# Attention probabilities transposed by VectorE blocks and DMAs inside SBUF, with contexts and outputs one step behind the scores

## The reference, cut to what matters

```python
def _cross_attention(q_in, kv_in, wq, bq, wk, bk, wv, bv, wo, bo, bias_k, bias_v):
    qh = (q_in @ wq + bq).reshape(b, q_len, H, K)
    kh = (kv_in @ wk + bk).reshape(b, t, H, K)
    vh = (kv_in @ wv + bv).reshape(b, t, H, K)
    kh = concatenate([kh, bias_k]); vh = concatenate([vh, bias_v])   # one learned key and value
    logits = jnp.einsum('bqhk,bthk->bhqt', qh, kh) / scale
    weights = jax.nn.softmax(logits, axis=-1)
    ctx = jnp.einsum('bhqt,bthk->bqhk', weights, vh).reshape(b, q_len, H * K)
    return ctx @ wo + bo
```

## Time and profile before

| | |
|---|---|
| median of 3 runs | 567.76 us |
| span of the profiled execution | 565.1 us; no time of its own is listed for it, so 2.7 us between it and the median stand for what lies around it |
| TensorE busy | 548.0 us, 97% |
| VectorE, ScalarE, GpSimd busy | 408.8, 315.1, 330.1 us (72%, 56%, 58%) |
| one step in the loop | 31.96 us |
| the chain that ended last | TensorE 82%, VectorE 11% |

### The profile page before, as it was taken

One profiled execution on the slowest core, in us unless ns is written; L12 is line 12 of the kernel. 1 busy time (PEld: TensorE's weight loads), 2 busy tenths in 40 slices (PEclk: granted clock), 3 DMA queues, 4 the chain that ended last, 5 costly groups with the idle time before them and its releaser, 6 DMA issues.

```text
span 565.1 us, 11067 instructions
## 1 busy us (share of the span) xinstructions
PE 548.0 (97%) x3665; PEld 492.8 (87%) x3665; DVE 408.8 (72%) x802; ACT 315.1 (56%) x707; POOL 330.1 (58%) x380
## 2 busy tenths in 40 slices
PE   7999999999999999999899999999999999999887
PEld 5979899898989899898879989898998989897787
DVE  3995776858586776858787685958768685858884
ACT  3475564747475564737266473746556474756432
POOL 3765655738364664837947393646557383746730
PEclk8999999999999999999999999999999999999999
DMA  7403030302102030301203020120203020000101
GB/s 240 128 22 73 19 74 0 78 15 56 37 22 70 18 75 0 74 20 54 77 19 94 1 74 19 43 50 19 74 0 92 1 71 22 0 19 2 38 1 38
DMA packets 26398, 25.85 MB, mean 46 GB/s; under 512 B 1530, under 2 KB 26254, under 8 KB 26382
## 3 DMA queue, kind: packets, MB, share of 16 engines
q1 hardware_dynamic: 26382, 25.64, 16.8%
HBM read 25.11 MB, written 0.52 MB: 45 GB/s over the span
## 4 chain that ended last, share of the span: by engine, by line
PE 82%; DVE 11%; issue 3%; DMA 1%; ACT 1%; POOL 0%; SPq 0%; DVEq 0%; ACTq 0%; POOLq 0%
PE ring L855 44%; PE ps_ctx L855 20%; PE acc L855 10%; PE ring L893 8%; DVE row_max L634 5%; DVE shift L640 2%; DMA probs<-ctx_in 1%; DVE z_sb L681 1%; ACT probs L469 1%; DVE x_sb L662 1%; DVE k_hi L841 0%; DVE cols L729 0%; DVE h_full L688 0%; DVE bn L670 0%; PE ring L930 0%
## 5 line engine op out<-in xcount | busy, mean ns | idle before, releaser
L336 POOL TENSOR_TENSOR v_lo<-v_sum,v_hi 128x512 fp32r<-128x512 f32 x64 | 82.2, 1295 | 129.1 <-ACT v_hi L448 127.3
L343 POOL TENSOR_SCALAR probs<-probs,inv 128x512 f32<-128x512 f32 x128 | 87.2, 694 | 63.9 <-DVE inv L656 63.9
L469 ACT ACTIVATE probs<-ring,shift 128x512 f32<-128x512 f32 x113 | 77.4, 685 | 32.3 <-DVE shift L640 28.7
L634 DVE TENSOR_REDUCE row_max<-ring 128x1 f32<-128x512 f32 x113 | 75.9, 685 | 11.6 <-PE ring L855 11.6
L448 ACT ACTIVATE v_hi<-v_sum 128x512 fp32r<-128x512 f32 x64 | 40.4, 632 | 77.4 <-DVE v_sum L611 77.4
L618 DVE TENSOR_TENSOR pT_lo<-ring,pT_hi 128x512 fp32r<-128x512 f32 x126 | 81.2, 684 | 3.0 <-ACT pT_hi L455 0.5
L455 ACT ACTIVATE pT_hi<-ring 128x512 fp32r<-128x512 f32 x126 | 69.9, 594 | 0.6 <-PE ring L893 0.5
L855 PE MATMUL ps_ctx<-pT_lo,v_hi 128*128 128x256 f32 x236 | 67.6, 286 | 0.0
L893 PE MATMUL ring<-ident,probs 128*128 128x128 f32 x504 | 65.8, 273 | 1.0 <-POOL probs L343 0.7
L855 PE MATMUL ps_ctx<-pT_hi,v_lo 128*128 128x256 f32 x236 | 66.1, 280 | 0.0
L855 PE MATMUL ps_ctx<-pT_hi,v_hi 128*128 128x256 f32 x236 | 66.1, 280 | 0.0
(11 more groups left out here) (153 smaller groups left out, 1537.3 us busy)
## 6 DMA issues: line engine op xcount, KB each, us to landing
wk_raw<-wk_in SPq DMA_DIRECT2D x17, 256.0 KB, 2.8
wv_raw<-wv_in SPq DMA_DIRECT2D x16, 256.0 KB, 2.7
vrows<-vrows_in SPq DMA_DIRECT2D x16, 256.0 KB, 4.8
wq_raw<-wq_in SPq DMA_DIRECT2D x16, 256.0 KB, 2.6
wo_raw<-wo_in SPq DMA_DIRECT2D x16, 256.0 KB, 2.7
wf_raw<-wf_in SPq DMA_DIRECT2D x7, 256.0 KB, 2.7
probs<-ctx_in SPq DMA_DIRECT2D x2, 512.0 KB, 5.2
x_sb<-x_in SPq DMA_DIRECT2D x1, 512.0 KB, 7.1
```

Source lines behind the costliest of these rows:

```text
L336: pool.tensor_tensor(v_lo[:, 2 * m:2 * m + 2, :], v_sum[:, m % 2, :].rearrange("p (t c) -> p t c", c=PW), v_hi[:, 2 * m:2 * m + 2, :].bitc ...
L343: pool.tensor_scalar(probs[:, u, q, :], probs[:, u, q, :], inv[:, u, q:q + 1], 0.0, ALU.mult, ALU.add).then_inc(p_ready, 1)
L469: act.activation(probs[:, u, q, :], ring[S_BANKS[where][QTB * u + q]][:], ACT.Exp, bias=shift[:, u, q:q + 1], scale=SCALE, accum_out=row_s ...
L634: dve.reduce_max(row_max[:, u, q:q + 1], ring[S_BANKS[where][QTB * u + q]][:], AX_X).then_inc(max_done, 1)
```

## The change

The pairs 0 to 6 of each layer no longer transpose on TensorE. `transpose_blocks(u)` on VectorE transposes 32x32 blocks of both tiles of a unit, 512 columns an instruction, from `probs` into a buffer `blocks` that holds two units. Then SyncE moves the blocks to their partitions: `move(pair, layer, n, first)` issues 16 DMAs from SBUF to SBUF, each of 32 partitions x 2 KB = 64 KB, for units 2n and 2n+1. They land in the room of the MLP's second weights (`wf2_hi`, `wf2_lo`), which are therefore loaded at the end. ScalarE rounds what has landed (`round_moved`, 1024 columns an instruction) and GpSimd makes the rest (`moved_rest`, 1024 columns) for units 0, 2 and 3, VectorE for unit 1. Half of unit 0's and 1's normalisation and all of unit 3's move from GpSimd to ScalarE. Shifts are now single columns.

The contexts and outputs of pair n run in step n+1, and the values of pair n are now projected in step n too. The first step of a layer is written apart and has no contexts, outputs or value projections. The last pair of a layer has a step with the contexts and outputs of the pair before and its own; it transposes its own probabilities on TensorE (`transpose_own`). Two more blocks of the MLP's first weights ride in `wq`.

```diff
+UNITS = [(0, 0), (1, 0), (0, 1), (1, 1)]
+NU = len(UNITS)
...
+BLK = 32
+QB = P // BLK
+RUN = 2 * CTB * QTB * BLK
...
+        blocks = sb("blocks", [P, QB, 2, CTB, QTB, BLK])
...
+        moved_to = [w[:].bitcast(F32).rearrange("p f d -> p (f d)").rearrange("p (i r) -> p i r", r=RUN) for w in (wf2_hi, wf2_lo)]
+        def moved(u):
+            part = moved_to[u // 2].rearrange("p i (u c q) -> p u c i q", u=2, c=CTB)
+            return part[:, u % 2, :, :, :]
...
+            def move(pair, layer, n, first):
+                done = pair - layer
+                if not first or layer > 0:
+                    for u in (2 * n, 2 * n + 1):
+                        hold(pT_split[u], done)
+                hold(blocks_ready, NU * done + 2 * (n + 1))
+                for i in range(QB):
+                    for g in range(QB):
+                        sp.dma_start(moved_to[n][BLK * g:BLK * (g + 1), i, :],
+                                     blocks[BLK * i:BLK * (i + 1), g, :, :, :, :].rearrange("p u c q b -> p (u c q b)")).then_inc(landed[n], LOAD)
+            def step(pair, layer, first=False, wq=True, wv=True):
+                sp.wait_ge(wk_split, pair + 2)
+                load_wk(pair + 2)
+                if first:
+                    sp.wait_ge(wq_split, pair + 2)
+                    load_wq(pair + 2)
+                else:
+                    sp.wait_ge(wo_split, pair)
+                    load_wo(pair)
+                move(pair, layer, 0, first)
+                move(pair, layer, 1, first)
+                if wq:
+                    sp.wait_ge(wq_split, pair + 3)
+                    load_wq(pair + 3)
+                if wv:
+                    sp.wait_ge(wv_split, pair + 2)
+                    load_wv(pair + 2)
...
+            def moved_rest(pair, layer, u):
+                pool.wait_ge(pT_rounded, NU * (pair - layer) + u + 1)
+                pool.tensor_tensor(pT_lo[:, u % 2, :, :].rearrange("p c (i q) -> p c i q", i=QB), moved(u),
+                                   pT_hi[:, u % 2, :, :].bitcast(F32).rearrange("p c (i q) -> p c i q", i=QB), ALU.subtract).then_inc(pT_split[u], 1)
...
+            def next_wv(pair):
+                pool.wait_ge(v_summed, NV * (pair + 1))
+                value_bias(pair + 1)
+                split_wv(pair + 1)
...
+            def step(pair, layer, first=False):
+                if first:
+                    next_wq(pair - 1)
+                else:
+                    pool.wait_ge(k_filled, NK * (pair + 1))
+                    split_wk(pair + 1)
                     pool.wait_ge(s_filled, NS * pair + 1)
+                    split_wo(pair - 1)
+                normalise(pair, 0, [1])
+                if not first:
+                    moved_rest(pair - 1, layer, 2)
+                normalise(pair, 1, [1])
+                if not first:
+                    value_rest(pair, 0)
+                    moved_rest(pair - 1, layer, 3)
+                    value_rest(pair, 1)
+                normalise(pair, 2, [0, 1])
+                next_wq(pair)
+                moved_rest(pair, layer, 0)
+                if not first:
+                    value_rest(pair, 2)
+                    value_rest(pair, 3)
+                next_wv(pair)
...
+            def round_moved(pair, layer, u, first=False):
+                act.wait_ge(landed[u // 2], QB * QB * LOAD * (pair - layer + 1))
+                if u < 2:
+                    if not first or layer > 0:
+                        act.wait_ge(o_filled, NU * (pair - 1) + u + 3)
+                else:
+                    act.wait_ge(o_filled, NU * pair + u - 1)
+                act.activation(pT_hi[:, u % 2, :, :].rearrange("p c (i q) -> p c i q", i=QB), moved(u), ACT.Copy).then_inc(pT_rounded, 1)
...
+            def transpose_blocks(pair, layer, u, first=False):
+                done = pair - layer
+                if u < 2:
+                    if not first or layer > 0:
+                        dve.wait_ge(landed[1], QB * QB * LOAD * done)
+                else:
+                    dve.wait_ge(landed[0], QB * QB * LOAD * (done + 1))
+                dve.wait_ge(p_ready_act, NU * pair + (u + 1 if u != 2 else 2))
+                dve.wait_ge(p_ready_pool, NU * pair + (u + 1 if u < 2 else NU))
+                for q in range(QTB):
+                    last = dve.transpose(blocks[:, :, u % 2, :, q, :].rearrange("p g c b -> p c g b"),
+                                         probs[:, u, q, :].rearrange("p (c g b) -> p c g b", g=QB, b=BLK))
+                last.then_inc(blocks_ready, 1)
...
+            def transpose_own(j):
+                u, q = divmod(j, 2)
+                for t in range(CTB):
+                    last = pe.transpose(ring[PT_BANKS[j]][:, t * P:(t + 1) * P], probs[:, u, q, t * P:(t + 1) * P], ident[:])
+                last.then_inc(own_filled, 1)
...
+            def step(pair, layer, first=False):
+                done = pair - layer
                 pe.wait_ge(q_split, NQ * pair + 1)
+                pe.wait_ge(k_split, NK * pair + (NK if first else 3))
+                scores(0, 0, "step")
+                pe.wait_ge(v_summed, NV * (pair + 1) if first else NV * (pair - 1) + 3)
+                scores(0, 1, "step")
+                if not first:
+                    pe.wait_ge(v_summed, NV * pair)
+                    pe.wait_ge(v_split, NV * (pair - 1) + 2)
+                    pe.wait_ge(pT_split[0], done)
+                    context(0, "step")
+                pe.wait_ge(q_split, NQ * (pair + 1))
+                pe.wait_ge(k_split, NK * (pair + 1))
+                scores(1, 0, "step")
+                scores(1, 1, "step")
+                if not first:
+                    pe.wait_ge(wv_split, pair + 1)
+                    project_v(0, "step")
+                    pe.wait_ge(exp_done, NS * pair + 1)
+                    pe.wait_ge(pT_split[1], done)
+                    context(1, "step")
+                    pe.wait_ge(o_split, NU * (pair - 1) + 1)
+                    pe.wait_ge(wo_split, pair)
+                    unit_output(0)
+                pe.wait_ge(exp_done, NS * pair + 2)
+                scores(2, 0, "step")
+                scores(2, 1, "step")
+                if not first:
+                    pe.wait_ge(exp_done, NS * pair + 3)
+                    project_v(1, "step")
+                    pe.wait_ge(o_split, NU * (pair - 1) + 2)
+                    unit_output(1)
+                pe.wait_ge(exp_done, NS * pair + 4)
+                pe.wait_ge(wq_split, pair + 2)
+                project_q(0, "step")
+                if not first:
+                    pe.wait_ge(v_summed, NV * pair + 1)
+                scores(3, 0, "step")
+                scores(3, 1, "step")
+                if not first:
+                    pe.wait_ge(exp_done, NS * pair + 5)
+                    pe.wait_ge(v_split, NV * pair)
+                    pe.wait_ge(pT_split[2], done)
+                    context(2, "step")
+                pe.wait_ge(exp_done, NS * pair + 6)
                 pe.wait_ge(wk_split, pair + 2)
                 project_k(0, "step")
+                if not first:
+                    pe.wait_ge(v_summed, NV * pair + 2)
                 project_k(1, "step")
+                if not first:
+                    pe.wait_ge(q_split, NQ * (pair + 1) + 1)
+                    pe.wait_ge(pT_split[3], done)
+                    context(3, "step")
+                    pe.wait_ge(o_split, NU * (pair - 1) + 3)
+                    unit_output(2)
                 pe.wait_ge(exp_done, NS * pair + 7)
+                project_q(1, "step")
+                pe.wait_ge(exp_done, NS * pair + 8)
+                project_k(2, "step")
+                if not first:
+                    project_v(2, "step")
+                    pe.wait_ge(k_split, NK * (pair + 1) + 1)
+                    project_v(3, "step")
+                pe.wait_ge(k_split, NK * (pair + 1) + 2)
+                project_k(3, "step")
+                if not first:
+                    pe.wait_ge(o_split, NU * pair)
+                    unit_output(3)
...
+                step(PAIRS * layer, layer, first=True)
+                with nc.Fori(PAIRS * layer + 1, PAIRS * (layer + 1) - 1, engines=(mybir.EngineType.PE,), hint_back_edge=True) as pair:
+                    step(pair, layer)
+                last_step(PAIRS * (layer + 1) - 1, layer, final=layer == LAYERS - 1)
```

858 lines of the change are left out of this document (436 added, 422 removed).

## The result

The changed kernel takes 629.75 us (629.38 to 630.57, 4 runs), against 567.67 us (566.6 to 568.83, 4 runs) of the kernel before beside it: a ratio of 1.109, 95% interval 1.107 to 1.111. It is 11% slower. I had predicted 558.0, with a range that ended at 588.

The account below looks back on a forecast made before the run. TensorE's queue was taken to bound the kernel before. First steps -19.7, twelve loop steps -22.3 and last steps +32.2 give -9.8 us: 565.1 becomes 555.3, or 558.0 with 2.7 us to the runs' median; range 545 to 588.

Parts of the forecast that it names:

- the move loop: Loop step: closed chain through two successive moves, ScalarE's rounding and exponentials, and VectorE's transposes; 27.3 us, with 2.8 us of slack.
- A move: SyncE's 16 issues 0.41 us apart, a landing of 1.9 and 0.15 to wake: 8.2 us (6.7 to 11.0).
- The stall that the sum leaves out: VectorE's two-operand sums of the inverses may be held behind a GpSimd rest, about 0.8 us; not priced.
- The mixed loop: Loop step: chain from unit_output(0) through VectorE, one move, ScalarE's rounding and GpSimd's splits; the longest, 30.1 us.
- The GpSimd row: Loop step: GpSimd's value rest, bias and weight splits that TensorE awaits at unit_output(0); 7.96 us, its loop 29.9.
- Block transposes: VectorE's transposes of 32x32 blocks, 512 columns an instruction: 0.60 us each, with no row to show it.
- The rival that made them slow: VectorE's transposes at 0.90 us each give 592 us, at 1.30 636; from +0.09 the gain is gone; chance 0.12.
- TensorE's work in a step: Loop step: TensorE's own matmuls without the transposes, 28.0 us.
- The first steps: First step of each layer: length set by the move, 22.1 us against 31.96, so -9.9 each.
- The last steps: Last step of each layer: +14.0 us of TensorE work and +2.1 of waiting; +32.2 in all after waits and cover.
- late moves: Rival: issues 0.54 us apart, landing after 2.7, so moves of 11.0, 2.8 more each; 597 us; chance 0.20.

Follow-up runs that it names:

- m1: Kernel before with eleven groups of transfers added behind its last store on SyncE, to time issues by kind; one run, 671.5 us in all.
- e7: Changed kernel with the buffer of transposed blocks doubled, so units 2 and 3 don't wait for the landing of units 0 and 1; 590.57 us.
- e2: Changed kernel with four transfers of 256 KB a move instead of 16, same bytes in the wrong places; 550.69 us, 0.971 of the kernel before.
- e9: Changed kernel with four spreading transfers a move, keys reordered where ScalarE reads scores, output weights split ahead of key weights; 542.68 us.
- e1: Changed kernel with eight transfers of 128 KB a move instead of 16, same bytes in the wrong places; 555.06 us, 0.979 of the kernel before.

## Why the prediction was wrong

The chain is the one that I had called *the move loop*, and one term of it failed: "Issues stand 0.41 us apart ... I take 0.41, since SyncE's queue is otherwise empty there". That price was read from loads out of DRAM. With both ends in SBUF the same queue issues 0.63 us apart, as m1 shows for the thing alone. Step by step, against my own numbers:

- *A move*: 8.2 us predicted, 11.4 measured. The pitch is 15 x (0.63 - 0.41) = 3.3 of it; the landing of 1.9 was right (2.0).
- *The move loop*: 27.3 us predicted, 34.6 measured. The two moves bring 6.4 of the 7.3. Another 0.6 lies between the landing and move 0, where I had 1.1 + 1.7 + 0.4 + 4.9 = 8.1 and the chain has 8.7, and 0.2 in the transposes of units 2 and 3 (3.0 for 2.8).
- *The stall that the sum leaves out*: it is there, and on the chain. In the timelines of GpSimd and VectorE of the changed kernel, the rest of unit 2 and the sum for the inverses:

```profile
204.73 2.41 POOL L377 TENSOR_TENSOR pT_lo<-wf_lo,pT_hi 128x1024 fp32r<-128x1024 f32 x1
```

```profile
202.66 0.15 DVE L764 TENSOR_TENSOR total<-row_sum,p_learned 128x2 f32<-128x2 f32 x1
...
206.00 1.15 DVE L764 TENSOR_TENSOR total<-row_sum,p_learned 128x2 f32<-128x2 f32 x1 [2.99 <-ACT probs L557]
```

  The sum of two columns takes 0.15 us by itself and 1.15 beside the rest, and ends at 207.15, where the rest ends (204.73 + 2.41 = 207.14). I had named 0.8 us and left it out, since I gave the move loop 2.8 us of slack. The rule that I cited for it from the Trainium skill's page "SBUF — State Buffer", section "SBUF: two separate sides", agrees with these rows. The rest of unit 1, which by that rule may be held too, takes 1.22 us in the median, as priced, and 1.56 at most.
- *The mixed loop*: 30.1 us predicted, as the longest. With moves of 11.4 my sum for it would be 33.3. So the loop that I had ranked last of four (30.1, 29.9, 28.0 and 27.3) led, because it holds two moves and takes the error twice. e7 takes just that loop apart, and then has 31.96 us a step: what binds there is 1.3 us less than my sum with the long move, and it goes through GpSimd's rest of unit 0 instead of VectorE's transposes of units 2 and 3.
- *The GpSimd row*, 29.9 us: right. e2 has 29.90 with short moves, and the two waits that I had named (`wo_lo`, `wv_lo`) are the ones there.
- *Block transposes*, 0.60 us: right. They take 685 ns, two of them 1.29, so 0.61 apart. The rival that made them slow did not happen, and the estimate of 1.24 us from the Trainium skill's page "VectorE: DVE Perf Modes" is not borne out.
- *TensorE's work in a step*, 28.0 us: right, 28.03 busy in e9.
- *The first steps*, 22.1 us predicted: 26.7 and 26.9. The longer move is 3.2 of the 4.7. By the copies such a step is 27.4 us here and 21.4 in e2, whose moves are 11.4 - (2.4 + 2.5) = 6.5 us shorter: so it does hold one move, as I had counted. The last 1.5 us stand ahead of the move. To the end of the transposes of unit 1 it takes 11.3 us for my 9.9, because the first maximum starts after 2.7, where I had 0.9; a copy of `cols`, 1.12 us on the chain, isn't in my list:

```profile
28.25 0.75 DVE q_lo L703
29.00 1.12 DVE cols L844
30.11 1.19 DVE row_max L755 x2
```

  TensorE's clock has no part in them, since from 27.52 to the move's end the chain doesn't pass TensorE. It costs something one step later. TensorE waits 8.15 us for `k_lo` at the end of the first step; ahead of the wait the granted clock is 1.00 and matmuls of 512 columns start 0.23 apart, and from 54 to 60 us, just behind it, the clock is 0.67, between its two levels of 1.2 and 2.4 GHz, and they start 0.43 apart until 56.76. The first loop step of each layer is 36.2 us by the copies, 1.6 over the others.
- *The last steps*: 1.9 and 7.0 us over my numbers. With e2's short moves the stretch from the last copy to the end is 69.9 us instead of 72.4, so 2.5 of the 7.0 are the moves. TensorE is busy 61.4 us in this stretch, where the 44.7 of before and the 14.0 that I added make 58.7, and its granted clock is 0.85 from 580 to 600 us, where before has 1.00 to the end. So the rest seems to be in part slower matmuls and in part an error of my count of waits; no run took them apart.

The sum then closes: the span is 73.5 us over the 555.3 of my sum, and twelve loop steps bring 55.8 (54.0 at 34.6 us each, the rest in the first one of each layer), the first steps 9.4, the last ones 8.9, the prologue -0.5.

The rival *late moves* had the mechanism and the sign, and still said 597 us. At its own move of 11.0 us the move loop is 27.3 + 2 x 2.8 = 32.9, no longer than the mixed loop that it was priced by. The 33 us that it lacks are some 12 x (34.6 - 32.9) = 20 in the loop, from the move's last 0.4 twice, the stall and the 0.2 above; 2 x 1.9 in the first steps; and the last steps. So its upper bound of a move was too low, because it was the longest pitch between loads out of DRAM, and my range, to 588, did not even reach it: I had argued 0.54 away as belonging to the start of the trace. What no row shows should be bounded further out than by the nearest rows when these are of another kind of transfer, and above all where it counts 28 times.

The Trainium skill, page "DMA: Bandwidth & Descriptors", section "Rules for kernel authors", says to coalesce many small transfers, and that under 64 KB one pays mostly overhead. Here that holds at 64 KB too, as e1 and e2 show (1 MB in 16 issues 11.4 us, in 4 issues 2.4 + 2.5). The same page, section "Issuing engines are not separate DMA queues", calls the time on the sequencer that starts a DMA usually small relative to the DMA itself. For one issue of 0.59 us against 2.0 to its landing that may still be said; in a row of them it is not so: 16 x 0.63 = 10.1 us of issuing, and then 2.0 to land.
